# Turning seven result chunks by VectorE and a round trip through DRAM instead of by identity matmuls, in a four-layer graph network on one core

## What is computed

```python
# layer 0: weights of each node's own, from a 16-wide embedding
x_g = [x, A@x, 2*A@(A@x) - x];  out = einsum('bnki,nkio->bno', x_g, w) + b
# layer 1: twice
z = relu((A @ z) @ weights[i])
# layer 2
out = x @ weight_self + (A @ x) @ weight_neighbor + bias
# layer 3: two supports, both of them adj
x1 = A @ x; x2 = 2*A@x1 - x;  out = concat(x, x1, x2, x1, x2) @ weight + bias
```

## Time and profile before

| | us |
|---|---|
| median of 3 runs | 1243.95 |
| lowest, highest | 1242.98, 1246.37 |
| span of the profiled execution | 1241.0 |
| TensorE matmuls busy in it | 1224.7 (99%), 5880 instructions |
| VectorE busy | 770.7 (62%), 1875 instructions |
| ScalarE busy | 212.8 (17%) |
| GpSimd busy | 66.7 (5%) |
| DMA | 81.34 MB, mean 66 GB/s |

### The profile page before, as it was taken

How to read it: one execution, slowest core, us unless ns; L and a number is a source line. 1 busy time by engine, 2 the same in 40 slices (tenths; PEclk the granted TensorE clock), 3 DMA queues, 4 the chain that set the end, 5 groups by cost and what they waited for, 6 DMA issues and landing times.

```text
span 1241.0 us, 16426 instructions
## 1 busy us (share of the span) xinstructions
PE 1224.7 (99%) x5880; PEld 1027.3 (83%) x5880; DVE 770.7 (62%) x1875; ACT 212.8 (17%) x388; POOL 66.7 (5%) x54
## 2 busy tenths in 40 slices
PE   7999999999999999999999999999999999999997
PEld 6888888888888887888888888888888888888877
DVE  5825898887768877788635564472246355644725
ACT  5722111120111101220111111020111111110101
POOL 0000000000000000000000010010000000100100
PEclk9999999999999999999999999999999999999999
DMA  9832112231213110101011123033001111230331
GB/s 343 336 102 61 31 47 77 61 103 36 61 56 102 52 39 22 48 22 43 15 35 35 34 69 68 17 106 82 1 26 43 35 35 34 69 68 17 85 70 37
DMA packets 142329, 81.34 MB, mean 66 GB/s; under 512 B 110096, under 2 KB 121104, under 8 KB 140432
## 3 DMA queue, kind: packets, MB, share of 16 engines
q1 hardware_dynamic: 142240, 80.19, 22.5%
HBM read 55.00 MB, written 25.17 MB: 65 GB/s over the span
## 4 chain that ended last, share of the span: by engine, by line
PE 94%; DVE 3%; DMA 1%; SPq 1%; issue 1%; ACT 0%; DVEq 0%
PE ps L727 30%; PE ps L728 30%; PE ps L831 22%; PE ps L745 8%; PE ps L766 2%; PE ps L767 2%; DMA raw<-in_at 1%; DVE ring L1103 1%; DVE nat L1103 1%; PE ps L739 1%; SPq L1149 0%; DVE sml L1043 0%; DMA ring_x<-y1d 0%; DVE sml L1034 0%; DVE nat L1038 0%
## 5 line engine op out<-in xcount | busy, mean ns | idle before, releaser
L727 PE MATMUL ps<-B,xs 128*128 128x512 f32 (+1 forms) x1680 | 656.3, 391 | 1.5 <-DVE xs L993 1.5
L728 PE MATMUL ps<-B,xs 128*128 128x512 f32 (+1 forms) x1680 | 649.4, 387 | 0.0
L727 PEld LDWEIGHTS ps<-B,xs 128*128 128x128 f32 x1680 | 315.8, 188 | 63.6 <-issue 1.6
L728 PEld LDWEIGHTS ps<-B,xs 128*128 128x128 f32 x1680 | 315.7, 188 | 61.8
L831 PE MATMUL ps<-Tw,xs 128*128 128x512 f32 x1280 | 309.0, 391 | 1.0 <-DVE ring L1103 1.0
L831 PEld LDWEIGHTS ps<-Tw,xs 128*128 128x128 f32 x1280 | 238.8, 188 | 54.3 <-DVE ring L1103 5.0
L981 DVE TENSOR_TENSOR ring<-ps,rrep 128x512 f32<-128x512 f32 (+1 forms) x95 | 64.6, 684 | 241.8 <-PE ps L728 230.7
L1103 DVE SCALAR_TENSOR_TENSOR nat<-ps,embn,nat 128x128 f32<-128x128 f32 x448 | 153.9, 344 | 43.2 <-PE ps L831 43.0
L1103 DVE SCALAR_TENSOR_TENSOR ring<-ps,embn,ring 128x128 f32<-128x128 f32 x512 | 175.7, 343 | 0.0
L745 PEld LDWEIGHTS ps<-W,ring 128*128 128x128 f32 x896 | 111.6, 191 | 7.5 <-DVE ring L981 1.9
L745 PE MATMUL ps<-W,ring 128*128 128x128 f32 x896 | 113.3, 275 | 0.7 <-DVE ring L981 0.6
(11 more groups left out here) (68 smaller groups left out, 546.4 us busy)
## 6 DMA issues: line engine op xcount, KB each, us to landing
raw<-in_at SPq DMA_DIRECT2D x13, 1024.0 KB, 16.3
td<-ring SPq DMA_DIRECT2D x32, 256.0 KB, 2.0
ring<-td SPq DMA_DIRECT2D x128, 64.0 KB, 2.6
ring<-in_xn SPq DMA_DIRECT2D x16, 256.0 KB, 2.8
ring_x<-in_xt SPq DMA_DIRECT2D x32, 128.0 KB, 3.1
ring_x<-y1d SPq DMA_DIRECT2D x32, 128.0 KB, 3.2
out<-nat SPq DMA_DIRECT2D x15, 256.0 KB, 2.4
y1d<-ring SPq DMA_DIRECT2D x14, 256.0 KB, 2.8
```

The lines of the kernel that those rows point to most:

```text
L727: pe.matmul(bank, x[:, 0, m, :], of, start=m == 0, stop=False)
L728: mm = pe.matmul(bank, x[:, 1, m, :], of, start=False, stop=ends and m == NT - 1)
```

## The change

Three chunks of the last kind and four of the first are moved from TensorE to the other way: all of pass 0 of pair 1, and the last chunk of pass 5 of the pairs 0, 2 and 3. TensorE keeps seven of its 14 chunks. In `second_pass0` a `turn` and a `back` are put for each of the four chunks of pair 1, `back` a quarter later than its `turn` and ahead of the next `turn`; the place of `weights0` in the list stays. In pass 5 a `back` is put behind `after` of the last chunk; its `turn` comes from the line that puts one for every chunk that isn't on TensorE. The tables of banks let the banks 0 to 3 go once `scale` has read them, and `turn` of pair 1's pass 0, which writes into `nat` over the pair's input, waits for the splits of that input.

```diff
 def on_pe(j, p, c):
 
-    return p == 0 and (j < 2 or c == 3) or p == 5 and c == 3
+    return p == 0 and (j == 0 or j > 1 and c == 3) or (j, p, c) == (1, 5, 3)
...
         put("after", j, p, 3)
+        if p == 5 and not on_pe(j, p, 3):
+            put("back", j, p, 3, 1)
         if norm:
...
             if i < 4:
                 put("scale", 1, 0, i)
+            if 0 < i < 5:
+                put("back", 1, 0, i - 1, 1)
+            if i < 4:
+                put("turn", 1, 0, i, 1)
             if 2 <= i < 6:
                 put("after", 1, 0, i - 2)
...
-            turn, held = [0, 1], {b: (s_evict, evict_at[after(1, 0, b)]) for b in range(2)}
+            turn, held = [0, 1], {b: (s_y, scale_at[Step("scale", 1, 0, b)]) for b in range(2)}
...
-            turn, held = [2, 3], {b: (s_evict, evict_at[after(1, 0, b)]) for b in (2, 3)}
+            turn, held = [2, 3], {b: (s_y, scale_at[Step("scale", 1, 0, b)]) for b in (2, 3)}
...
             for s in STEPS:
-                if s.kind == "after" and s.p == 0 and s.j < 2:
+                if s.kind == "after" and (s.j, s.p) == (0, 0):
                     nbank_of[s, "turn"] = bank_of["prod", s.j, 0, s.c]
...
                             dv.wait_ge(s_y, scale_at[Step("scale", j, p, c)])
-                            if p == 0:
+                            if (j, p) == (1, 0):
+                                dv.wait_ge(s_hi, split_at[Step("split", 1, 0, c)])
+                                dv.wait_ge(s_lo, split_at[Step("split", 1, 0, c)])
+                            elif p == 0:
                                 dv.wait_ge(s_z[n][c], 16)
```

## The result

The changed kernel takes 1256.18 us (median of 4 runs, 1255.92 to 1258.94) where the kernel before takes 1244.16 (4 runs, those of the table and one more). The ratio is 1.0097, with a 95% interval of 1.0086 to 1.0109: 12.0 us slower, where 8.3 were forecast. The profiled execution has a span of 1254.3 us. That is 13.3 us over the one before, but 1.7 of these lie behind the last instruction on VectorE, where the last result is being stored: from its end to the end of the span it is 4.1 us here and 2.4 before.

What follows compares the result with a forecast made beforehand. TensorE was taken as the bound (94% of the chain). `T` beginning 9.6 us later, less 1.3 us from the late three, gave net +8.3 us on the median 1243.95: 1252.3 us, range 1247.5 to 1254.5.

Steps and rivals of the forecast that it cites:

- The bound: TensorE, 94% of the chain: matmuls removed gain in full, waits put in lose in full, nothing later absorbs either.
- the late three: Last chunks of pass 5, pairs 0, 2, 3: 1.3 us gained, ways back hidden by 3.4 us; rival that they miss 0.05.
- What comes off TensorE: Identity matmuls of seven chunks: four in pair 1 worth 1.9 us, three in pass 5 worth 1.3, together 3.2 us.
- The mechanism: Pair 1: round trips on SP's queue delay w2, then VectorE's weights and splits; TensorE stands 9.5 us before pass 1.
- The queue: SP's queue before `weights0`: 5.2 us for each of the second to fourth round trips, w2 issued at 102.2 instead of 86.18.
- Landing and the way through the weights: w2 takes 5.4 us to land, at 107.6; VectorE's L1054 starts then, pair 1's first split is ready at 114.6.
- The clock: After TensorE's 9.5 us rest, first matmuls run slow, costing 2.1 us; rival that the rest costs no clock 0.27.
- the second gate: Before `T`: `loadx` waits for finished weights, then `fetch` and casts, so `T` can begin at 120.3; alone adds 0.3 us.
- The choice of the upper end: Slow clock's price after the rest put between 0 and 2.1 us; the forecast took 2.1.
- After `T`: `T` begins at 122.1 instead of 112.47, +9.6 us; the sum adds nothing behind it but 1.3 us given back.
- the likeliest case: The forecast itself, whole kernel: net +8.3 us, 1252.3 us, with the slow clock counted; chance 0.50.
- My high end: Top of the range, 1254.5 us: waits of 2.85 us and all four stores in the way add 2 us.

Runs made afterwards that it cites:

- loads_first: Changed kernel with SP's two loads of w01 and w2 moved ahead of the first turn of pair 1: 1249.17 us, ratio 1.0041 to the kernel before.
- two_chunks: Changed kernel, but only chunks 0 and 1 of pair 1's pass 0 turned by VectorE, 2 and 3 on TensorE: 1242.46 us, ratio 0.9985.
- busy_gap: Changed kernel with 48 extra matmuls, results unused, where TensorE idles before pair 1's pass 1: 1251.81 us, ratio 1.0062 to the kernel before.
- reordered: Changed kernel, SP's queue reordered: turns and stores at once, only one way back before the w01/w2 loads, own semaphores for the turns: 1241.28 us, ratio 0.9971.
- late_only: Kernel before with only the last chunk of pass 5 of pairs 0, 2 and 3 turned by VectorE: 1242.08 us, ratio 0.9985.
- three_chunks: Changed kernel, but only chunks 0 to 2 of pair 1's pass 0 turned by VectorE, chunk 3 on TensorE: 1250.18 us, ratio 1.0046.

## Why the prediction was right and where it was wrong

**The bound.** Right: nothing absorbed the gap, and nothing absorbed the gain of the late three.

**What comes off TensorE.** Right: 3.2 us forecast. With the queue in order the kernel gains 3.1 us by the medians (2.1 to 5.1 by the interval), and the late three alone 1.4 by the marks.

**The mechanism.** Right in every step: w2 late behind four round trips, VectorE standing for it with the splits queued behind, TensorE standing for the splits. loads_first took the first gap away and two_chunks showed the threshold. The prediction had allowed w2 until 90.6 us without a loss, which is 91.6 where two chunks' identity matmuls are still in TensorE's way; 93.5 cost 0.4 us, so it lies at 93.1 in this trace, 1.5 us later than forecast.

**The sizes.** Here the forecast failed: 8.3 us against 12.0, and 1256.18 is above the range's 1254.5. Three terms of the sum were too small: the issue of w2 (102.2 us, measured 103.9), its landing and the way from there to TensorE (12.4 us, measured 12.9), and everything behind `T`, which the sum put at nothing but the late three's gain (measured 1.2 us of further loss). The steps one by one:

- *The queue.* "5.2 us for each of the second to fourth" was 5.2 to 5.4, the first turn went out 0.5 us later than I had it (0.35 of it because this execution was later already), the two stores behind the last way back took 1.3 us for 1.0, and between the last store and w01 lie another 0.5 us. w2 went out at 103.9 instead of 102.2: 1.7 us short.
- *Landing and the way through the weights.* w2 landed 5.7 us after its issue, not 5.4, and from there to TensorE it was 7.2 us, not 7.0: 0.5 us short.
- *The clock.* Right. The slow matmuls were to cost 2.1 us and cost 2.0. As the second gate stands close behind, only 1.8 of them were to count (122.1 against 120.3), and 1.8 is what busy_gap got back. The choice of the upper end was right.
- *The second gate.* It was to be ready at 120.3 and not to bind behind slow matmuls, and didn't: `prep` ended at 122.4, `T` began at 124.3. What I had not seen is its other key, the stores to `y1d`; it was covered in the changed kernel and laid bare by loads_first.
- *After `T`.* I let everything behind `T` move as one. `T` was 11.8 us late, and by the marks the distance to the kernel before grew to 13.0 before the late three took off 1.4. Half of the growth arises between 215 and 250 us; the other half arises between 568 and 598 us and was not traced to a step. There VectorE waits for a `fetch` through ScalarE's cast. The same step in the kernel before (L1081), in reordered (L1095) and in busy_gap (L1093):

```profile
239.56 0.69 DVE L1081 TENSOR_TENSOR xs<-ring_x,xs 128x512 fp32r<-128x512 f32 x1 [3.33 <-ACT xs L926]
```

```profile
238.28 0.69 DVE L1095 TENSOR_TENSOR xs<-ring_x,xs 128x512 fp32r<-128x512 f32 x1 [4.38 <-ACT xs L937]
```

```profile
247.86 0.69 DVE L1093 TENSOR_TENSOR xs<-ring_x,xs 128x512 fp32r<-128x512 f32 x1 [2.67 <-ACT xs L935]
```

The longer this wait, the more TensorE loses a few us later: the distance changes by +1.0 us in reordered and by -0.7 in busy_gap, and by +0.6 in the changed kernel, whose wait here is 3.90. In all nine traces it changes by as much as the wait differs from 3.33, to 0.05 us. SP begins to issue this `fetch` at the same distance from the marks in all nine, in the kernel before here:

```profile
234.65 0.61 SPq L1234 DMA_DIRECT2D ring_x<-in_xt  x1
```

From there to ScalarE's cast it is 3.6 us in busy_gap, 4.3 before, 4.8 in the changed kernel and 5.3 in reordered. So what differs is how long this one `fetch` takes from its issue to its landing. Each kernel has one trace, and whether it goes with the kernel or with the execution was not settled. It isn't a matter of the gap, since reordered has none.

So the likeliest case was the right one, with its terms too small by 2.2 us up to `T` and by 1.2 us behind it; another 0.2 is the median before, which rose with its fourth run. My high end allowed 2 us for the queue and nothing for landing or for layer 0, so it was too near.

**The late three.** Right: hidden, by the waits of late_only.

## What to carry to other kernels

On a queue that issues in order, a round trip costs what stands behind it, so for each transfer already there ask who waits for its issue and who waits for its landing. The same seven turns cost 12 us in one order of the queue and bring 3 us in another. Issue what others wait for first, start the outward transfers, and only then wait for them to come back (reordered had room for one way back ahead of the loads); this takes a semaphore of its own for each transfer under way. And take away one gate, and look for the next on the same queue before counting the gain: loads_first removed the gap it aimed at and got back 7 of 15 us.

## What the runs showed of the hardware

TensorE's granted clock falls while it rests, and the fall outlasts the rest. It fell in a rest of 11.2 us (0.57 and then 0.50 in the windows above) and also in shorter ones: behind 5.33 us in three_chunks, and behind 4.82 us in loads_first, whose window reads 0.50:

```profile
115.00:120.00 5.00, 4.61 (x11) 3.72 (x12) 0.28 (x1) 0.62 (x1) 0.00 (x0) 0.50 0.37 121
```

Behind 0.40 us (two_chunks) and 1.70 us the spacing stayed short. The 2 us or so that it costs come on top of the rest itself, whether that is 5 or 11 us long. Forty-eight matmuls whose results nobody reads kept the granted clock at 1.00 through the gap and gave 1.8 of them back. The Trainium skill, page "TensorE: Matmul & The Clock Gate", Part 1, says that an idle array goes back to the lower level and that sustained work brings it up again, and these runs agree with it: 0.50 behind the rests of 4.82 and 11.2 us, and in the changed kernel full speed again from 121 us on, with TensorE at work since 116.81. In the first microseconds of the kernel before, though, the page of the profile has the clock as full where the matmuls are 0.43 us apart, the spacing that goes with 0.50 behind the rest of 11.2 us. So in the first microseconds I go by the spacing and not by the clock row.
